# Four heads' score matmuls in one issue instead of two pairs, and GpSimd's normalising ahead of its weight splitting in half of layer 0's steps

## What is computed

```
layer 0: twice x = x + cross_attention(layer_norm(x), ctx)    # 16 heads of 128, one extra key per head
         x = x + gelu(layer_norm(x) @ w_fc1) @ w_fc2
layer 1: a recurrent mixer over 256 tokens and a small feed-forward
layer 2: q = x@Wq (16 heads of 16), k, v from layer_norm(ctx)
         attn = softmax(q k^T * 0.25 + mask);  x = x + tanh(gate) * (attn v) @ Wo
layer 3: q = x@Wq + bq (32 heads of 8), k, v from ctx (8 heads, each shared by 4 query heads)
         attn = softmax(q k^T / sqrt(8) + mask);  x = layer_norm(x + (attn v) @ Wo + bo)
```

## Time and profile before

| what | value |
|---|---|
| runs without profile | 1202.15 us median of 3 (1202.07 to 1203.07) |
| profiled execution | 1202.93 us, its span 1200.9 us |
| PE busy | 1118.7 us, 93% of the span, x7404 matmuls |
| DVE, ACT, POOL busy | 808.3 (67%), 646.7 (54%), 684.2 us (57%) |
| layer 0 | until about 720 us |
| last layers | from about 889 us to the end |
| TensorE's granted clock | mean 0.983; 1.00 throughout 880 to 1190 us |

### The profile page before, as it was taken

One profiled execution on the slowest core, in us unless ns is written; L12 is line 12 of the kernel. 1 busy time (PEld: TensorE's weight loads), 2 busy tenths in 40 slices (PEclk: granted clock), 3 DMA queues, 4 the chain that ended last, 5 costly groups with the idle time before them and its releaser, 6 DMA issues. The chain is left out here.

```text
span 1200.9 us, 20667 instructions
## 1 busy us (share of the span) xinstructions
PE 1118.7 (93%) x7404; PEld 883.7 (74%) x7404; DVE 808.3 (67%) x1986; ACT 646.7 (54%) x1451; POOL 684.2 (57%) x746
## 2 busy tenths in 40 slices
PE   5999999999999999999999988989689999999996
PEld 4888788988898888898878973444456767667674
DVE  6677666686667766767765757688656655666774
ACT  3655655656556555655565211622235656687764
POOL 3666665675656656656676303476016655565874
PEclk9899999999999999999999997999799999999999
DMA  6101210221022102210220300000020100000000
GB/s 212 55 25 65 71 53 19 71 71 53 19 71 71 54 18 71 71 54 19 71 71 19 93 5 13 1 1 0 1 62 2 37 1 2 1 2 1 11 10 19
DMA packets 35338, 46.97 MB, mean 39 GB/s; under 512 B 3931, under 2 KB 22308, under 8 KB 35237
## 3 DMA queue, kind: packets, MB, share of 16 engines
q1 hardware_dynamic: 34866, 45.00, 11.6%
q10 hardware_dynamic: 370, 0.64, 0.2%
HBM read 44.59 MB, written 1.05 MB: 38 GB/s over the span
## 5 line engine op out<-in xcount | busy, mean ns | idle before, releaser
L379 POOL TENSOR_TENSOR a_prob<-a_prob,a_inv_total 128x512 f32<-128x512 f32 x128 | 144.2, 1126 | 192.4 <-DVE a_inv_total L684 192.4
L2027 POOL TENSOR_TENSOR scores<-scores,neg_max 128x512 f32<-128x512 f32 x144 | 147.5, 1041 | 79.5 <-DVE neg_max L1898 79.3
L574 ACT ACTIVATE a_prob<-psum,a_neg_max 128x257 f32<-128x257 f32 x256 | 119.2, 472 | 101.7 <-DVE a_neg_max L681 100.4
L1821 ACT ACTIVATE prob_T<-psum 128x512 f32<-128x512 f32 x192 | 113.1, 600 | 35.5 <-PE psum L1742 34.0
L1742 PE MATMUL psum<-ident,scores 128*128 128x128 f32 x768 | 117.8, 280 | 1.5 <-POOL scores L2027 1.5
L1742 PEld LDWEIGHTS psum<-ident,scores 128*128 128x128 f32 x768 | 85.7, 141 | 36.8 <-issue 16.3
L1898 DVE CUSTOM_DVE_ANT_0 scores<-psum,ctx_rows 128x256 f32<-128x256 f32 x256 | 93.7, 420 | 18.6 <-PE psum L1742 9.2
L688 DVE TENSOR_TENSOR a_probT_lo<-psum,a_probT_hi 128x512 fp32r<-128x512 f32 x128 | 88.0, 687 | 24.3 <-ACT a_probT_hi L578 24.0
L503 PE MATMUL psum<-ident,a_prob 128*128 128x128 f32 x512 | 77.3, 273 | 14.6 <-POOL rows_bc L383 12.6
L681 DVE TENSOR_REDUCE a_neg_max<-psum 128x2 f32<-128x514 f32 x128 | 87.4, 683 | 1.2 <-PE psum L425 1.2
L503 PEld LDWEIGHTS psum<-ident,a_prob 128*128 128x128 f32 x512 | 60.6, 140 | 32.7 <-DVE a_q_lo L730 13.4
(11 more groups left out here) (358 smaller groups left out, 3319.1 us busy)
## 6 DMA issues: line engine op xcount, KB each, us to landing
wk_raw<-in_L_xattn_wk SPq DMA_DIRECT2D x16, 512.0 KB, 6.3
wq_raw<-in_L_xattn_wq SPq DMA_DIRECT2D x16, 512.0 KB, 5.6
wv_raw<-in_L_xattn_wv SPq DMA_DIRECT2D x16, 512.0 KB, 3.7
wo_raw<-in_L_xattn_wo SPq DMA_DIRECT2D x16, 512.0 KB, 4.0
ctx_rows<-in_ctx SPq DMA_DIRECT2D x3, 512.0 KB, 4.2
x_rows<-in_x SPq DMA_DIRECT2D x2, 512.0 KB, 9.9
ctx_rows<-in_mask_Bx1xSxS_ff SPq DMA_DIRECT2D x1, 1024.0 KB, 5.4
out_dram<-x_rows SPq DMA_DIRECT2D x4, 256.0 KB, 2.1
```

The costliest lines, as they stand in the source:

```text
L379: pool.tensor_tensor(prob[:, m % 4, :, 0:S], prob[:, m % 4, :, 0:S], rtot[:, m % 4, :].unsqueeze(2).to_broadcast([P, 2, S]), ALU.mult)
L574: act.activation(prob[:, m % 4, q, 0:S + 1], s_bank(g)[:, q, 0:S + 1], ACT.Exp, bias=negm[:, m % 4, q:q + 1], accum_out=tot[:, m % 4, q:q ...
L1821: act.activation(pT[:, i % PT, :], t_bank(i), ACT.Exp, scale=1.0 if on_scalar(i) else -1.0).then_inc(exp_ok, 1)
L2027: pool.tensor_tensor(sc[:, i % SC, :, :], sc[:, i % SC, :, :], m[:, i % SC, :].unsqueeze(2).to_broadcast([P, 2, S]), ALU.subtract).then_in ...
```

## The change

In the last layers an S entry now does four heads, on all four row groups, with each head in its own bank of the same four. `LEAD` goes from 4 pairs to 2 fours; the entry s = i // 4 + 2 stands behind T(i) for `i % 4 == 1`, where one of the two pairs stood. It waits until all four banks are read: heads up to 4s - 1. Behind T(4n+1) the four heads 4n+8 to 4n+11 wait for `max(4n + 7)`. DVE's list places maxima up to `at + 6` for odd `at` too. In layer 0, `norm(6)` and `norm(7)` stand ahead of the splitting of `v` in the steps with `i % NQ` of 1 and 2.

```diff
@@ stage_layer0, GpSimd
                     if i % NQ == 2:
                         h_low(event_of(i))
+                    if i % NQ in (1, 2):
+                        norm(6)
+                        norm(7)
                     pool.wait_ge(acc_full, USE[i, 'V3'] + 1)
                     cut_half('v', i + 1, 0)
-                    norm(6)
+                    if i % NQ not in (1, 2):
+                        norm(6)
                     cut_half('v', i + 1, 1)
-                    norm(7)
+                    if i % NQ not in (1, 2):
+                        norm(7)
@@ last_layers_orders
-LEAD = 4
+LEAD = 2
...
-    pe = [('F', p) for p in opening] + [('S', 0), ('S', 1)] + [('F', p) for p in second] + [('S', 2), ('S', 3)]
+    pe = [('F', p) for p in opening] + [('S', 0)] + [('F', p) for p in second] + [('S', 1)]
...
-        if i % 2 and i // 2 + LEAD < HEADS // 2:
-            pe.append(('S', i // 2 + LEAD))
+        if i % 4 == 1 and i // 4 + LEAD < QUADS:
+            pe.append(('S', i // 4 + LEAD))
...
-                    max_to(at + (5 if at % 2 else 6))
+                    max_to(at + 6)
@@ scores, on PE
-                    l, b, e = head_of(2 * s)
+                    l, b, e = head_of(4 * s)
...
-                    if s >= 2:
-                        pe.wait_ge(s_read, 2 * s - 2)
+                    if s:
+                        pe.wait_ge(s_read, 4 * s)
                     at = b % 2 * S
                     for q in range(2):
                         for k in range(sh.passes):
-                            for i in (2 * s, 2 * s + 1):
+                            for i in range(4 * s, 4 * s + 4):
@@ maximum, on DVE
-                    dve.wait_ge(s_full, i // 2 + 1)
+                    dve.wait_ge(s_full, i // 4 + 1)
```

More of the change, by code:

```diff
@@ L1462, in last_layers_orders @@
     for kind, p in pe:
-        if kind == 'S' and p == 2:
+        if kind == 'S' and p == 1:
             act.append(('shift', 2))
@@ L1713, in scores @@
                 def scores(s):
-                    l, b, e = head_of(2 * s)
+                    l, b, e = head_of(4 * s)
                     sh = SMALL[l]
-                    if s < 2:
+                    if s == 0:
                         pieces = [p for (kind, p), bank in bank_of.items() if kind == 'F' and bank < 4]
                         landed(pe, [max((p for p in pieces if evictor(p) == who), key=number.get) for who in ('act', 'dve')])
-                    if e % 4 == 0 and b % 2 == 0:
+                    if b % 2 == 0:
                         landed(pe, stack_pieces(l, b // 2, e // 4))
-                    if s >= 2:
-                        pe.wait_ge(s_read, 2 * s - 2)
+                    if s:
+                        pe.wait_ge(s_read, 4 * s)
                     at = b % 2 * S
```

## The result

The changed kernel takes **1217.68 us** (median of 4 runs, 1216.57 to 1218.04) against 1202.11 us for the kernel before, measured beside it: a ratio of 1.0132 with a 95% interval of 1.0117 to 1.0147. It is slower by 15.6 us. I had forecast 8.3 us slower, with a range that ended at 1216: the direction came, the size did not.

A forecast was written before the change was run, and what follows sets the result against it. PE, busy 93% of the span, was taken to bound the kernel; the last layers 15.7 us slower from waits for DVE's maxima, less 7.5 from layer 0, gave 8.2 us slower, 1210.4 us; range 1200 to 1216.

The forecast's parts named there:

- What PE saves: Last layers: each dropped S entry saves PE 0.60 us in layer 3, 0.84 in layer 2; 32.6 us without gaps.
- The circle: Last layers: S waits for DVE's maxima, which need transposes behind the previous S; layer 3's 31 fours take 18.3 us more.
- Four streams dearer than two: Rival, S entries: a round of four row groups takes 1.3 times one of two; 7.4 us more, 1217.8 us; 8%.
- The bare circle: Layer 3 fours without pieces that DVE evicts at these places: 4.53 us from one S entry to the next.
- The clock: Last layers: PE idle some 20 to 40 us before S entries; no cost named for the granted clock.
- Layer 2, the opening and the end: Layer 2's 14 fours 1.6 us less in all, the opening 1.0 us less; nothing named for the end.
- Layer 0: Norms ahead of v's splitting: four steps of remainder 2 each 1.88 us shorter, remainder 1 unchanged; 7.5 us saved.
- The readers only cancel: Rival, last layers: DVE's chain eats only what PE saves, leaving layer 0's 7.5 us gain; 1194.7 us; 13%.
- layer 0 gives all of its wait: Rival, layer 0: DVE's inverse comes earlier without GpSimd's splits beside it, saving 12.6 us; 1205.3 us; 8%.
- PE sets the pace: Rival, whole kernel: the change does what it says, 32.6 + 7.5 us less; 1162 us; 1%.
- The range: Whole kernel: 1200 to 1216 us, leaving out most of the cancelling case and the dear streams.

The follow-up runs named there:

- experiment 9: Changed kernel with an eighth buffer for scores in layer 3 (the place of layer 2's dead V weights), nothing moved: 1211.25 us, ratio 1.0084.
- experiment 4: Changed kernel with each four-head S entry moved from behind a four's second transpose to behind its last, DVE's order following: 1179.52 us, ratio 0.9821.
- experiments 3: Kernel before, pair entries kept, with every second entry's wait raised to all four readers and DVE's evictions one maximum later: 1236.41 us, ratio 1.0297.
- experiment 10: Changed kernel with an eighth scores buffer in layer 3 and most of DVE's layer 3 evictions one maximum later: 1191.44 us, ratio 0.9912.
- experiment 5: Changed kernel with useless identity transposes filling PE's waits before S in 20 fours of layer 3: 1210.18 us, ratio 1.0072.
- experiment 8: Changed kernel with the sums moved from behind the scores to behind T(4n+2), ahead of the piece there: 1228.53 us, ratio 1.0223.
- experiment 6: Changed kernel with S entries moved behind each four's last transpose, and inside each entry two heads' matmuls before the other two's: 1179.32 us, ratio 0.9812.

## Why the prediction was right in its sign and short in its size

- **What PE saves**: right, and hidden by the circle. The slot of four heads is 0.44 us in layer 3 and 0.67 in layer 2, as one pair's was the earlier trace rows. With the changed kernel's order and no wait, in experiment 9, a four saves 0.58 us where 0.60 was named. The order of experiment 4 saves only the slot, 0.43.
- **Four streams dearer than two**: the rival with 1217.8 us named almost the measured time and is wrong all the same; no slot grew, where 1.3 times would have been 0.56 us in layer 3.
- **The circle**: right as the mechanism (experiments 3, 4, 9 and 10), and right to 0.1 or 0.2 us in all classes but one four. Idle time in front of S was 44.4 us, a little over the 20 to 40 named. By pieces in a four:

| pieces | named, us | measured, us |
|---|---|---|
| one OT | 5.36 | 5.36 five times, 5.47 |
| two OT's | 5.86 | 5.75, 5.81, 5.85, and 6.32 (four 15) |
| V and OT | 7.0 | 6.90 |
| OP at T(4n-2) | 8.00 | 8.02, 7.92 |
| OP at T(4n) | 7.91 | 8.05 |
| OP of layer 2 | 6.75 | 6.95 |
| K | 7.4 | 7.59 |
| two Q's | 8.7 | 8.75 |
| stack pieces | 6.4 | 6.32, 6.31 |

- **The bare circle**: 4.53 named, 4.66 to 4.67 measured in seven fours. ("No four can be shorter" was too strong: in experiment 5 three of them took 4.45.) The term left out is the second wait for a buffer: in the rows of the result, DVE's second head starts at 1073.90 and not at 1073.69, since its T(4n-1) stands behind a stack piece. That is 0.21 us more; the last head and the release of PE took 0.10 less than the 0.92 named. I had checked the buffer for the first maximum alone. Experiment 8 missed for the same reason.
- **The clock**: the step that failed. The prediction spoke of PE idling for 20 to 40 us and priced only the idling; what the idling does to the clock it put at nothing. The sum for layer 3 was 176.6 us, and 183.4 were measured. Of these 6.8 us, 5.16 are four stretches at 1.2 GHz behind long waits, as experiment 5 shows, about 1.1 are the twelve bare fours, and the rest is small change. Without the 5.16 us the changed kernel would have taken about 1212.5 us, inside the range. The Trainium skill (TensorE: Matmul & The Clock Gate, A second HAM failure mode: psum-queue depth-cycling) tells of a kernel in which short idle times of TensorE between groups of matmuls, as it cycled through PSUM banks, made the clock swing between its two levels. The trace agrees in that: four stretches at half clock behind waits of 1.9 to 2.9 us.
- **Layer 2, the opening and the end**: 0.9 us less where 1.6 were named; the opening gave nothing instead of 1.0, for S 1 now waits 0.67 us for DVE's first maxima; behind the 31 fours 1.75 us came back that I had not counted. These nearly cancel, so the 6.6 us by which the spans differ more than named (14.8 against 8.2) are about layer 3's 6.8.
- **Layer 0**: right. 1.89, 1.84, 1.87 and 1.92 us in the four steps, 1.88 named; the steps of remainder 1 grew by 0.01 to 0.10 us. Together 7.5, and by itself the part measured 6.0 us faster (4.9 to 8.4 by its interval).
- **The readers only cancel, layer 0 gives all of its wait, PE sets the pace**: none came.
- **The range**: its bound upwards was too near. Both of the circle's bounds were on the short side, and I had none for what a long wait does to the clock of the engine that waits.

## What to carry to other kernels

When buffers of two stages are merged into fewer, larger ones, list for every reader which earlier step frees its buffer, follow all of them and not the first, and see whether they close a circle with the writer; then issue the large step where all of its readers' buffers are already free. Here that is one condition in PE's list, with DVE's list following, and it turns 1.3% slower into 1.8% faster (layer 0's gain of about 0.6% is in both). Price a new wait on TensorE twice: once as idle time, and once as the half-clock time that may follow it.

## What the hardware showed that I had not expected

- The clock fell behind idle times of 1.90, 2.28, 2.79 and 2.88 us on a TensorE that was otherwise busy; each time for 3.41 us, which cost 0.8 to 1.6 us. In the same profile it held behind the 2.34 us shown above and behind waits of 1.74 and 1.84:

```profile
1027.12 0.51 PE L1734 MATMUL psum<-k_stack,q_stack 32*128 32x256 f32 x8 [1.84 <-DVE neg_max L1903]
...
1041.66 0.51 PE L1734 MATMUL psum<-k_stack,q_stack 32*128 32x256 f32 x8 [1.74 <-DVE neg_max L1903]
```

  The length of the wait alone does not decide. In experiment 8 the clock fell behind the same wait of 1.74 us (at 1044.73), and held behind those of 2.79 and 2.28. In experiment 9 it held behind these two as well, and in experiment 10 it fell behind 2.19 us and held behind 2.10. Experiment 5 shows that idleness in front of S brings the stretches; which of the waits does it stays open.

- In experiment 6 the matmuls of heads 2 and 3 stood in the program behind two more of heads 0 and 1, and still started within 17 ns of the first: a matmul whose row group is busy does not hold back those of another. Eight of them took 0.45 us, as in the order by fours. That reading rests on start times and the slot; which head each start belongs to the trace does not tell.
